# Grouped-query attention in fp32, one core: two of five probability chunks turned by VectorE and a DRAM buffer, and the work of every engine put in another order

## What is computed

```python
q = jnp.einsum('bsd,ed->bse', x, Wq).reshape(bsz, seqlen, HQ, D)
k, v = ...
q = _rope(_rmsnorm(q, q_norm_w), pos)
k = _rope(_rmsnorm(k, k_norm_w), pos)
k_all = jnp.concatenate([k_cache[block_table].reshape(bsz, L, HK, D), k], axis=1)
v_all = jnp.concatenate([v_cache[block_table].reshape(bsz, L, HK, D), v], axis=1)
scores = jnp.einsum('bqhd,bkhd->bhqk', q, k_all) * SCALE
probs = jax.nn.softmax(jnp.where(valid, scores, -1e30), axis=-1)
o = jnp.einsum('bhqk,bkhd->bqhd', probs, v_all).reshape(bsz, seqlen, HQ * D)
return jnp.einsum('bse,de->bsd', o, Wo)
```

## Time and profile before

| | us |
|---|---|
| median of 3 runs (1351.86 to 1352.45) | 1351.88 |
| span of the profiled execution, first to last instruction | 1349.8 |
| PE busy | 1342.4 |
| DVE busy | 1040.8 |
| ACT busy | 843.2 |
| POOL busy | 713.6 |
| mean DMA rate, GB/s | 125 |

### The profile page before, as it was taken

How to read it: one execution, slowest core, us unless ns; L and a number is a source line. 1 busy time by engine, 2 the same in 40 slices (tenths; PEclk the granted TensorE clock), 3 DMA queues, 4 the chain that set the end, 5 groups by cost and what they waited for, 6 DMA issues and landing times.

```text
span 1349.8 us, 24930 instructions
## 1 busy us (share of the span) xinstructions
PE 1342.4 (99%) x7812; PEld 1191.3 (88%) x7812; DVE 1040.8 (77%) x2131; ACT 843.2 (62%) x2217; POOL 713.6 (53%) x972
## 2 busy tenths in 40 slices
PE   9999999999999999999999999999999999999999
PEld 8888888888889998889888989888888888888887
DVE  7988777877787778777877787778778887748546
ACT  7676566666566556666666666566665785545444
POOL 7767465646554655565555555555555652305111
PEclk9999999999999999999999999999999999999999
DMA  5566325522552264126413641364222164354532
GB/s 201 172 185 198 87 82 173 145 63 78 187 127 59 78 201 134 38 84 206 130 31 108 203 109 31 113 210 128 79 48 48 63 191 140 125 183 141 187 141 78
DMA packets 170746, 168.11 MB, mean 125 GB/s; under 512 B 129856, under 2 KB 137664, under 8 KB 159936
## 3 DMA queue, kind: packets, MB, share of 16 engines
q1 hardware_dynamic: 164928, 131.21, 33.3%
q0 software_dynamic: 5760, 36.18, 8.1%
HBM read 133.81 MB, written 33.55 MB: 124 GB/s over the span
## 4 chain that ended last, share of the span: by engine, by line
PE 98%; POOL 1%; DVE 1%; ACT 1%; issue 0%; POOLq 0%; DVEq 0%
PE ps L64 27%; PE ps L63 27%; PE ps L65 27%; PE ps L1131 10%; PE ps L1109 2%; PE ps L1153 1%; PE ps L2038 1%; PE ps L1103 1%; PE ps L2071 0%; PE ps L2070 0%; PE ps L2024 0%; PE ps L2023 0%; PE ps L1332 0%; DVE at_scores L897 0%; PE ps L2009 0%; ACT at_mask L601 0%
## 5 line engine op out<-in xcount | busy, mean ns | idle before, releaser
L502 POOL TENSOR_SCALAR at_probs<-at_probs,at_row_inv 128x640 f32<-128x640 f32 x256 | 211.8, 828 | 151.1 <-DVE at_row_inv L903 150.9
L605 ACT ACTIVATE at_pT_hi<-ps 128x512 fp32r<-128x512 f32 x320 | 186.5, 604 | 101.1 <-PE ps L65 50.9
L897 DVE CUSTOM_DVE_ANT_0 at_scores<-ps,at_mask,at_inv_rms 128x640 f32<-128x640 f32 x256 | 220.2, 879 | 31.7 <-PE ps L65 30.8
L653 ACT ACTIVATE at_probs<-at_scores,at_neg_max 128x640 f32<-128x640 f32 x256 | 211.9, 836 | 51.0 <-DVE at_neg_max L897 51.0
L845 DVE TENSOR_TENSOR at_pT_lo<-ps,at_pT_hi 128x512 fp32r<-128x512 f32 x320 | 212.6, 686 | 25.7 <-ACT at_pT_hi L605 20.7
L63 PE MATMUL ps<-ds_hi,x_hi 128*128 128x512 f32 (+1 forms) x564 | 192.7, 342 | 0.0
L65 PE MATMUL ps<-ds_hi,x_lo 128*128 128x512 f32 (+1 forms) x564 | 192.0, 340 | 0.0
L648 ACT ACTIVATE at_square<-ps 128x128 bf16<-128x128 f32 x256 | 67.1, 276 | 166.7 <-DVE a_raw L876 149.9
L1131 PE MATMUL ps<-ident,at_probs 128*128 128x128 f32 x1280 | 160.6, 273 | 0.0
L63 PE MATMUL ps<-at_kT_hi,ds_lo 128*128 128x320 f32 x512 | 158.1, 309 | 1.6 <-DVE at_neg_max L897 1.6
L65 PE MATMUL ps<-at_kT_hi,ds_lo 128*128 128x320 f32 x512 | 158.2, 309 | 0.0
(11 more groups left out here) (215 smaller groups left out, 3379.6 us busy)
## 6 DMA issues: line engine op xcount, KB each, us to landing
kT_pages<-shared SPq DMA_DIRECT2D x16, 1024.0 KB
kv_raw<-kT_pages SPq DMA_DIRECT2D x60, 256.0 KB, 4.0
v_pages<-shared SPq DMA_DIRECT2D x14, 1024.0 KB
kv_raw<-v_pages SPq DMA_DIRECT2D x56, 256.0 KB, 4.1
sw_wgu_raw<-in_sw_gu SPq DMA_DIRECT2D x22, 512.0 KB, 3.3
staging<-in_L_cond_Wo SPq DMA_DIRECT2D x8, 1024.0 KB, 4.8
staging<-in_L_cond_Wq SPq DMA_DIRECT2D x7, 1024.0 KB
sw_b_raw<-in_sw_bgu SPq DMA_DIRECT2D x88, 64.0 KB, 2.8
```

Of the source, the lines that this page charges most:

```text
L502: pool.tensor_scalar(probs[:, h, :], probs[:, h, :], row_inv[:, h:h + 1], 1.0, ALU.mult, ALU.mult).then_inc(probs_done, 1)
L605: act.activation(out, src, ACT.Copy).then_inc(done, 1)
L653: act.activation(probs[:, h, :], scores[h % 2][:], ACT.Exp, bias=neg_max[:, h:h + 1], scale=-1.0, accum_out=row_sum[:, h:h + 1]).then_inc( ...
L897: dve.tensor_tensor_reduce(out=scores[h % 2][:], in0=slot(h), in1=mask[:, b, :], scale=inv_rms[b % 2][:, h:h + 1], scalar=3.0e38, op0=ALU. ...
```

## The change

For 62 of the 64 rounds (`by_moves`: all but the very first and the very last) TensorE transposes only chunks 0 to 2. Chunks 3 and 4 (the last 128 cached keys and the 128 new ones) take another way: after each `normalise`, VectorE transposes the 32 by 32 squares of the head's last 256 columns (`turn_squares`, one instruction for each head, SBUF to SBUF, into `turned`); SP writes `turned` to a DRAM buffer of 512 KB (`move_turned`), waits for it, and reads it back in four DMAs of 32 partitions each into `pT_raw`, which puts the squares in their places; ScalarE and VectorE then split the two chunks out of `pT_raw` in SBUF, where they read PSUM before. In the other orders: TensorE runs the output projection of the round before behind the twelve transposes, scores 2 and 3 and the key projection ahead of products 2 to 4, and the transposes of the queries of (g2, b2) at the round's end; ScalarE's and VectorE's lists follow that; GpSimd issues the gather of pages at the start of a round and rotates the queries ahead of the keys; SP begins each round with `move_turned`. Three semaphores are merged into one (`passed`), two others into one, and the descriptor buffer of the indirect DMAs is set to 8192.

```diff
 
 P = 128
+SQ = 32
...
 
+        MOVED = 2
         SCORE_PARTS = [(0, KEYS // 2), (KEYS // 2, KEYS)]
...
         mask_bias = sb("mask_bias", [P, B])
+        turned = sb("turned", [P, NQ, MOVED, G, SQ])
+        pT_raw = sb("pT_raw", [P, NQ, MOVED, G, SQ])
...
+        def preceding(g, b):
+            return (g, b - 1) if b else (g - 1, B - 1)
+
+        def by_moves(g, b):
+
+            return not (isinstance(g, int) and (g, b) in ((0, 0), (HK - 1, B - 1)))
+
+        def turned_in_psum(g, b, c):
+
+            first = isinstance(g, int) and (g, b) == (0, 0)
+            return c + 1 if first else upto(g, b, KC - MOVED, MOVED + c + 1)
+
+        def moved_chunk(c):
+
+            return pT_raw[:, :, c - (KC - MOVED)].rearrange("p a h r -> p h a r")
+
+        def moved_count(g, b):
+
+            return g * (B // 2 * (NQ + 1) * 16) + (b // 2 + b % 2) * (NQ + 1) * 16
 
...
+            def move_turned(g, b):
+
+                wait_apart(sp, turned_done, upto(g, b, G), passed)
+                sp.dma_start(turned_rows, turned[:].rearrange("p k c h r -> p (k c h r)")).then_inc(pT_moved[b % 2], 16)
+                wait_apart(sp, pT_moved[b % 2], moved_count(g, b) - NQ * 16, passed)
+                for k in range(NQ):
+                    sp.dma_start(pT_raw[k * SQ:(k + 1) * SQ].rearrange("i a c h r -> i a (c h r)"),
+                                 turned_rows.rearrange("(a i) (k n) -> k i a n", a=NQ, k=NQ)[k]).then_inc(pT_moved[b % 2], 16)
...
             def group(g, last):
                 for b in range(B):
                     g2, b2 = following(*following(g, b))
+                    if by_moves(g, b):
+                        move_turned(g, b)
...
@@ -540,29 +575,26 @@
                     if by_row(g2):
                         pool.wait_ge(v_cache_done, b + 1)
                         gather(b2, v_rows, v_raw, v_loaded)
-                    if more2:
-                        key_scale(g2, b2)
+                    if first and 2 <= b < 6:
+                        stage_pages(g, b - 2)
+                    if not first and not last and 1 <= b < 5:
+                        stage_pages(g, b - 1)
                     if b == B - 3 and not last:
                         qkv_group(g + 1, DC)
                         qkv_group(g + 1, DC + 1)
                     if more2:
-                        rotate_k(g2, b2)
+                        key_scale(g2, b2)
                     if b == 0:
                         wo_group(g, 0)
                         wo_group(g, 1)
                     if first and b == 1:
                         stage_first_keys(1)
-                    if first and 2 <= b < 6:
-                        stage_pages(g, b - 2)
-                    if not first and not last and 1 <= b < 5:
-                        stage_pages(g, b - 1)
-                    if more2 and not (last and b == B - 3):
+                    if more2:
                         rotate_q(g2, b2)
+                        rotate_k(g2, b2)
                     if more:
                         for h in range(G):
                             normalise(g1, b1, h)
-                    if last and b == B - 3:
-                        rotate_q(g2, b2)
                     if more2:
...
                     act.wait_ge(pv_done, upto(g, b, KC, c - RING + 1))
-                hi(pT_hi[c % RING][:], bank(probs_bank(b, c)), pT_in_psum, upto(g, b, KC, c + 1), pT_hi_done[c])
+                if by_moves(g, b) and c >= KC - MOVED:
+                    hi(pT_hi[c % RING][:].rearrange("p (h a r) -> p h a r", h=G, a=NQ), moved_chunk(c), pT_moved[b % 2], moved_count(g, b), pT_hi_done[c])
+                else:
+                    hi(pT_hi[c % RING][:], bank(probs_bank(b, c)), pT_in_psum, turned_in_psum(g, b, c), pT_hi_done[c])
...
+                    if more:
+                        exps(g1, b1, 0)
+                        exps(g1, b1, 1)
                     if b == B - 3 and not last:
                         qkv_group(g + 1, 0)
                         qkv_group(g + 1, 1)
-                    if more2 and not (last and b == B - 3):
-                        squares(g2, b2)
-                    if more:
-                        exps(g1, b1, 0)
-                        exps(g1, b1, 1)
-                    if last and b == B - 2:
-                        dense.part_hi(act, 1, 1)
-                    hi(oT_hi[:], bank(o_bank(b)), pv_done, upto(g, b, KC, KC), oT_hi_done)
+                    if by_moves(g, b):
+                        for c in range(KC - MOVED, KC):
+                            probs_T(g, b, c)
                     if more:
                         exps(g1, b1, 2)
+                        exps(g1, b1, 3)
+                    if more2:
+                        squares(g2, b2)
...
             def probs_T(g, b, c):
-                lo(pT_lo[c % RING][:], bank(probs_bank(b, c)), pT_hi[c % RING][:], pT_hi_done[c], upto(g, b, 1, 1), pT_done)
+                if by_moves(g, b) and c >= KC - MOVED:
+                    l, h = (t[c % RING][:].rearrange("p (h a r) -> p h a r", h=G, a=NQ) for t in (pT_lo, pT_hi))
+                    lo(l, moved_chunk(c), h, pT_hi_done[c], upto(g, b, 1, 1), pT_done)
+                else:
+                    lo(pT_lo[c % RING][:], bank(probs_bank(b, c)), pT_hi[c % RING][:], pT_hi_done[c], upto(g, b, 1, 1), pT_done)
+
+            def turn_squares(g, b, h):
+
+                wait_apart(dve, probs_done, upto(g, b, G, h + 1), passed)
+                dve.transpose(turned[:, :, :, h, :].rearrange("p k c r -> p c k r"),
+                              probs[:, h, (KC - MOVED) * P:KEYS].rearrange("p (c k i) -> p c k i", c=MOVED, k=NQ)).then_inc(turned_done, 1)
...
+                    started = not (first and b == 0)
+
+                    if started:
+                        attended(*preceding(g, b))
+                    if more:
+                        queries(g1, b1)
+                    probs_T(g, b, 0)
                     if b == B - 2 and not last:
                         qkv_group(g + 1, 2)
-                    probs_T(g, b, 0)
+                    if more and started:
+                        new_values(g1, b1)
+                        cached_values(g1, b1)
                     probs_T(g, b, 1)
+                    if b == B - 2 and not last:
+                        qkv_group(g + 1, 3)
+                    if more and started:
+                        cached_keys(g1, b1)
+                    if started:
+                        add_y(*preceding(g, b), last and b > 0)
+                    probs_T(g, b, 2)
                     if more:
-                        queries(g1, b1)
                         new_keys(g1, b1)
-                    probs_T(g, b, 2)
                     if first and b < B - 2:
                         table(b + 2)
-                    if b == B - 2 and not last:
-                        qkv_group(g + 1, 3)
-                    for c in range(3, KC):
-                        probs_T(g, b, c)
...
+                    if not by_moves(g, b):
+                        for c in range(KC - MOVED, KC):
+                            probs_T(g, b, c)
...
+                    if more:
+                        inverse(g1, b1, 0)
+                        mask_and_max(g1, b1, 2)
+                        inverse(g1, b1, 1)
                     if b == 0:
...
                     if more:
-                        mask_and_max(g1, b1, 2)
-                        inverse(g1, b1, 1)
-                    attended(g, b)
+                        mask_and_max(g1, b1, 3)
+                    if by_moves(g, b):
+                        probs_T(g, b, 3)
+                    if more:
+                        inverse(g1, b1, 2)
+                    if by_moves(g, b):
+                        probs_T(g, b, 4)
...
+                    if more:
+                        inverse(g1, b1, 3)
...
+                    if more and by_moves(g1, b1):
+                        for h in range(G):
+                            turn_squares(g1, b1, h)
+                    if b == B - 3 and not last:
+                        qkv_group(g + 1, 1)
...
+                pe.wait_ge(pT_done, upto(g, b, KC, max(c + 1, KC - MOVED)))
                 three_pass(pe, bank(o_bank(b)), v_hi[j][:, c, :], v_lo[j][:, c, :], pT_hi[c % RING][:], pT_lo[c % RING][:], c == 0, c == KC - 1).then_inc(pv_done, 1)
...
+                    started = not (first and b == 0)
+                    for c in range(KC - MOVED):
+                        probs_T(g, b, c)
+                    if started:
+                        output(*preceding(g, b))
                     if more:
-                        queries(g1, b1)
                         new_keys(g1, b1)
-                    for c in range(2, KC):
-                        probs_T(g, b, c)
-                    times_v(g, b, 0)
-                    times_v(g, b, 1)
+                    if not by_moves(g, b):
+                        for c in range(KC - MOVED, KC):
+                            probs_T(g, b, c)
```

(20 more changed lines are left out.)

187 lines of the change are left out of this document (84 added, 103 removed).

## The result

The changed kernel takes 1379.2 us (median of 4 runs, 1376.5 to 1379.5), the kernel before 1351.9 beside it: ratio 1.0195, 95% interval 1.0181 to 1.021. The forecast was 1325, range 1299 to 1348: wrong in its sign, and outside its range.

What follows compares the result with a forecast made beforehand. The prediction took TensorE, busy all of each 16.60 us round, as the bound: -52.1 + 11.2 + 2.9 + 6.3 + 5 = -26.7 us, with the offset to the 1351.9 us median kept, 1325 us; range 1299 to 1348.

Steps and rivals of the forecast that it cites:

- -0.84 us a round for eight transposes: TensorE, 62 rounds: eight of twenty transposes removed at 0.105 us each, round 16.60 to 15.76 us, -52.1 us in all.
- Transposes at 0.35 us (0.20 to 0.81): VectorE: each of four 128x256 transposes a round takes 0.35 us, 1.4 us a round, fitting by its sum.
- 0.18 us of wait on the divisions: Round's end: TensorE ready at 4.1 us, GpSimd's divisions done at 4.3; 62 waits, +11.2 us (0 to 25).
- b = 0, +2.9 us in all: Rounds b = 0: a weight subtraction before the last maximum ends the divisions 0.42 us later, seven times (0 to 5).
- It just fits: Round's end: low part of the attended values ready at 5.0 us, output projection needs it at 5.06.
- b = 5, +6.3 (3 to 9): Rounds b = 5: ScalarE copies and a second VectorE subtraction delay the round, 7 times 0.9 us.
- come some 5 us later in the round and are used a round later: SP's loads for the sequence after next, behind the DRAM way: later but not needed until a round later, costed at nothing.
- First and last head, +5 (0 to 10): First and last head: extra VectorE instructions no longer hide, about ten rounds at 0.5 us.
- The way through DRAM at nothing: Turned chunks land 9 to 10 us after the last transpose, ScalarE wants them about 10.8 us into the round: no cost.
- the late chunks: Rival: turned chunks come back late, ScalarE stalls before exponential 2, 1393 us at 12.0 us; chance 0.10.
- The transposes do not take the ports: Denies the rival that VectorE's transposes lock the port pair against divisions, about 0.85 us a round, 1378 us; chance 0.05.
- The first rival: TensorE still never waits, the 0.18 us and most other waits vanish: 1300 us; chance 0.25.

Runs made afterwards that it cites:

- the mended version with the loop written out: Changed kernel with VectorE's heads 1 to 6 written out, dense weight load and adapter-number reads early, two first-head edits: 1337.3 us, ratio 0.9881 of the kernel before.
- the run with orders alone: Changed kernel with `by_moves` False everywhere, so TensorE turns all five chunks in the new order, without the DRAM way: 1523.1 us, ratio 1.1261.
- two edits together: GpSimd's weight subtractions ahead of round 5's page staging, VectorE's second angle half later, against the version with three mends (1339.9 us): 1337.3 us.

## Why the prediction was wrong

Its steps, each against what was measured:

- **-0.84 us a round for eight transposes: right.** The shortest rounds of the change, in heads 0 and 7, where VectorE's code is written out, take 15.79 and 15.85 us, against 15.76. The rule of the Trainium skill that it weighed against this (VectorE: DVE Perf Modes, "Rules for kernel authors"), that such a transpose belongs on TensorE, did not hold for this kernel: VectorE's four transposes, 0.43 us each, are free as long as it has room, and the mended version with the loop written out is 1.2% faster than the kernel before.
- **Transposes at 0.35 us (0.20 to 0.81): low.** They take 0.43 in the mean:
```profile
L960 DVE STREAM_TRANSPOSE at_turned<-at_probs 128x256 f32<-128x256 f32 x248 | 99.8, 426 | 22.5 <-POOL at_probs L537 18.8
```
- **0.18 us of wait on the divisions: right in kind, low in size.** TensorE's weight loads waited 11.3 us in 46 of the 48 rounds of heads 1 to 6, 0.25 each, released by the division on GpSimd, as foretold. With VectorE written out 1.7 us in 7 rounds are left. So the chain of six steps was good to 0.2 us and no better, and it had no term for what the loop costs a plain round, 0.17 us. Whether the loop's register instructions do that or its code loads, no run separates.
- **b = 0, +2.9 us in all: this step failed.** "By the same steps the divisions end 0.42 later" costs the work of that round and nothing else. The weight's share was 0.67 a head (16.55 against 15.88), not far off. What it missed is the branch, in front of the subtraction of which the same prediction says "It just fits": 2.6 to 4.2 us in each of five rounds, 16.3 in all, which it had put at nothing. The kernel before shows no price for a branch, and I did not count how many instructions the transposes add to the loop, or bound what a longer body may cost.
- **b = 5, +6.3 (3 to 9): too dear, within its bounds.** It is 0.57 each, 4.0 in all, but round 6 costs 0.72 each as well, which no term had.
- **SP's loads "come some 5 us later in the round and are used a round later": this step failed too.** It is true of keys and values. SP runs in order, and two other things stood in the same queue: the dense weight, wanted in the very same round (8.0 us), and eight reads of numbers, 14 us long, that had been hidden because SP ran ahead: before, they were over 32 us ahead of the last round (9.0 us). A list of all that stands behind the new DMAs in SP's queue would have found both; the prediction has no such list.
- **First and last head, +5 (0 to 10): mis-sized.** Seven rounds at -0.66 and one projection fewer should have made head 0 7.4 us shorter; it is 4.0 longer. Three of these 11 are round 0, which stays on TensorE and takes 18.7 us without a projection where it took 18.4 with one: that is the price of the new order without moves, which the run with orders alone shows in every round. Head 7 is too low as well: apart from its round 2 its rounds up to the last one should be 4.6 shorter and are 0.9 longer. Together that is 16 us beyond the other terms, where the bound was 10.
- **The way through DRAM at nothing: right from head 1 on.** ScalarE waited 1.4 us for turned chunks in all of heads 1 to 6. In the median it lands sooner than I took from the earlier trace rows:
```profile
turned_rows<-at_turned SPq DMA_DIRECT2D x62, 512.0 KB, 2.6
at_pT_raw<-turned_rows SPq DMA_DIRECT2D x248, 128.0 KB, 3.2
```
In head 0 it was wrong: writes took up to 4.1 us and the last read 5.9 to 8.35 in three rounds at least, beside gathers, and the chain runs through them.

The spans differ by 24.9 us where the forecast had -26.7: 51.6 us have to be found.

| measured less forecast, each line with the forecast's terms for its own rounds | us |
|---|---|
| branch, first rounds of heads 2 to 6 | 16.3 |
| dense weight, round 2 of head 7 (23.10 against 16.46) | 6.6 |
| numbers read late, the last part (284.8 against 277.1) | 7.7 |
| heads 1 to 6 otherwise | 7.6 |
| head 0 | 10.5 |
| head 7 otherwise, up to its last round | 5.1 |
| last round with the mask rows in time, and the start | 2.9 |
| less the forecast's own 5 for the first and last head | -5 |

They add up to 51.7. The 7.6 of heads 1 to 6 are plain rounds at 16.05 instead of 15.94 (5.3), round 6 (3.7) and round 0 (0.5), less 2.0 that round 5 was taken too dear. The first three lines are shown by runs that take the cause away; of head 0, two edits together gave 2.6 back, and the rest of its line and head 7's stay open.

Of the rivals, the late chunks mattered in head 0, and not in the plain rounds for which they were priced. The transposes do not take the ports: three of them took 1.26 us beside a division, and one alone takes 0.45. The first rival, a TensorE that never waits, did not happen either. The one on the slower side should have been "what was hidden by an engine's running ahead".

## What to carry to other kernels

Before adding instructions to a loop body, count the engine's instructions in it, register and semaphore ones too, and look at the profile's instruction queue: if loads of code appear inside a loop that had none, see what stands behind the branch, and who waits for it. A wait put into an in-order queue that used to run ahead shows everything that the running ahead had hidden; list all that stands behind it, up to the end of the program, with when it is wanted. And a chain worked out to 0.2 us is worth nothing beside a stall of 2.6 us that no row of the old trace could show: where the change touches a loop, give that a term with bounds.

## What the runs showed of the hardware

- VectorE's loop body of 321 instructions runs without code loads, those of 361, 386 and 401 are loaded again in each turn, 9 to 12 transfers in two turns. Behind the branch VectorE stands for 2.1 to 2.8 us. With the kernel before, the rounds inside the body keep their length (16.60 to 16.63 us). Written-out code is loaded too, 19 transfers in heads 1 to 6, and VectorE stands nowhere for them.
- A TensorE that was idle for 2.4 us came back at 1.2 GHz for 3.5 us in two cases, and at full clock in three.
- With VectorE's loop written out, its waits against constants and no register instructions left, a plain round of the change got 0.17 us shorter. Its code loads in heads 1 to 6 fell from 34 to 19 as well, and which of the two does it is not shown. The kernel before gained nothing by the same.
- Reading one number from DRAM into a register costs SP about 1.8 us (eight in 14.1).
- A GpSimd subtraction pair and a VectorE subtraction, all on SBUF, met at 122.1 us: the pair took 2.56 us, 1.3 each as always, and VectorE's subtraction 3.09 instead of 0.68: it ended 0.55 us behind the pair.
